# Packed half tiles in the down stage, grouped part copies of the weights, and a reordered opening

## What is computed

```
xn = layernorm(x)
gate = xn @ Wg.T ; up = xn @ Wu.T          # 2752 x 1024 each
inter = silu(gate) * up                     # 4096 x 2752
ffn = inter @ Wd.T                          # Wd: 1024 x 2752
attn = xn + softmax(q q^T / sqrt(1024)) q   # q: 4 x 1024 per feature column
out = x + attn * silu(ffn)
```

## Time and profile before

| | |
|---|---|
| three runs | 2485.27, 2484.89, 2483.41 us, median 2484.89 |
| profiled execution | 2484.12 us, span 2482.3 us |
| PE busy | 2407.4 us, 97% of the span, 11214 matmuls |
| DVE, ACT, POOL busy | 65%, 41%, 3% |
| mean granted TensorE clock | 0.989 of full speed |

### The profile page before, as it was taken

How to read it: one execution, slowest core, us unless ns; L and a number is a source line. 1 busy time by engine, 2 the same in 40 slices (tenths; PEclk the granted TensorE clock), 3 DMA queues, 4 the chain that set the end, 5 groups by cost and what they waited for, 6 DMA issues and landing times.

```text
span 2482.3 us, 30225 instructions
## 1 busy us (share of the span) xinstructions
PE 2407.4 (97%) x11214; PEld 1107.6 (45%) x11214; DVE 1605.8 (65%) x2757; ACT 1006.0 (41%) x1145; POOL 83.4 (3%) x72
## 2 busy tenths in 40 slices
PE   2899999999999999999999999999999999999999
PEld 2444444444444444444444444444444444444444
DVE  8888787668998867788888886565422422421431
ACT  8877777777878443544445421110010000001001
POOL 0000000000000000000000000000010011001001
PEclk7899999999999999999999999999999999999999
DMA  6855776657766895566655544248867767777764
GB/s 244 258 173 181 246 250 205 199 178 255 247 237 213 282 360 194 174 218 216 217 193 197 200 146 142 94 181 316 322 259 315 298 245 290 301 284 287 299 258 165
DMA packets 172127, 579.52 MB, mean 233 GB/s; under 512 B 17648, under 2 KB 42912, under 8 KB 154188
## 3 DMA queue, kind: packets, MB, share of 16 engines
q1 hardware_dynamic: 136716, 289.21, 34.4%
q10 hardware_dynamic: 35264, 288.37, 29.9%
HBM read 388.76 MB, written 188.75 MB: 233 GB/s over the span
## 4 chain that ended last, share of the span: by engine, by line
PE 88%; DVE 4%; ACT 3%; issue 3%; DMA 2%; POOL 0%; SPq 0%; ACTq 0%; POOLq 0%; DVEq 0%
PE ps L1813 56%; PE ps L1958 31%; ACT arena L792 1%; DMA arena<-in_x 1%; PE ps L1886 1%; ACT arena L805 1%; PE ps L1767 1%; DVE arena L1334 0%; DVE arena L1265 0%; DVE arena L1423 0%; DVE arena L1308 0%; DMA arena<-in_gu 0%; ACT arena L957 0%; DVE arena L1355 0%; POOL arena L761 0%
## 5 line engine op out<-in xcount | busy, mean ns | idle before, releaser
L1813 PE MATMUL ps<-arena 128*128 128x512 f16 x7152 | 1554.0, 380 | 12.4 <-ACT arena L995 6.8
L1813 PEld LDWEIGHTS ps<-arena 128*128 128x128 f16 x7152 | 700.1, 98 | 853.6 <-ACT arena L995 7.3
L1958 PE MATMUL ps<-arena 128*128 128x512 f16 x3696 | 797.9, 379 | 0.0
L792 ACT ACTIVATE arena<-arena,bias_t 128x2048 f32<-128x2048 f32 (+3 forms) x288 | 525.0, 1830 | 79.8 <-DMA arena<-in_dn 68.7
L1958 PEld LDWEIGHTS ps<-arena 128*128 128x128 f16 x3696 | 361.6, 98 | 436.1
L1423 DVE TENSOR_TENSOR arena<-arena 128x512 f16<-128x512 f32 x364 | 243.2, 684 | 11.7 <-ACT arena L957 10.4
L1221 ACT ACTIVATE arena<-arena,e_d 128x512 f32<-128x512 f32 x48 | 34.6, 721 | 424.3 <-DVE arena L1732 219.4
L1005 ACT ACTIVATE arena<-ps,gate_back 128x512 f32<-128x512 f32 x84 | 57.1, 680 | 305.6 <-PE ps L1813 305.5
L761 POOL TENSOR_TENSOR arena<-arena 128x512 f32<-128x512 f32 x64 | 81.5, 1280 | 2384.6 <-DMA arena<-in_xt 2076.2
L1708 DVE SCALAR_TENSOR_TENSOR arena<-arena,sc 128x512 f32<-128x512 f32 x192 | 129.8, 744 | 0.0
L1015 ACT ACTIVATE arena<-arena,gate_back 128x512 f32<-128x512 f32 x84 | 60.4, 720 | 161.5 <-DVE arena L1596 152.1
(11 more groups left out here) (108 smaller groups left out, 1167.4 us busy)
## 6 DMA issues: line engine op xcount, KB each, us to landing
isc<-arena SPq DMA_DIRECT2D x308, 256.0 KB, 2.6
arena<-wdsc ACTq DMA_DIRECT2D x28, 2816.0 KB, 10.2
arena<-isc ACTq DMA_DIRECT2D x28, 2816.0 KB, 18.1
arena<-xnsc SPq DMA_DIRECT2D x48, 1024.0 KB, 8.6
wsc<-arena ACTq DMA_DIRECT2D x21, 1792.0 KB, 6.7
arena<-in_x SPq DMA_DIRECT2D x48, 512.0 KB, 5.6
arena<-in_gu ACTq DMA_DIRECT2D x43, 512.0 KB, 4.6
wdsc<-arena SPq DMA_DIRECT2D x77, 256.0 KB, 2.1
```

The lines of the kernel that those rows point to most:

```text
L792: a_.activation(buf, src, ACT.Prelu, bias=bias_t[:, i:i + 1], scale=scale, alpha=alpha).then_inc(ramps, 1)
L1813: ins = t_.matmul(ps[:, bank, :], wreg[:, b, w, wa, k, :], xreg[:, j, o, k, xa, :], start=start and (k, wa, xa) == (0, 0, 0), stop=stop an ...
L1958: ins = t_.matmul(ps[:, bank, :], ring_w[b][:, k, wa, g, :], ring_i[b][:, k, xa, :], start=first and (k, wa, xa) == (0, 0, 0), stop=r not ...
```

## The change

Five things change together.

1. **Packed half tiles.** In the down stage, for combinations 1, 2 and 3, the last slice's 64 live rows are put twice into the 128 rows. SP stores high parts of the results in rows 0 to 63 and low parts in rows 64 to 127 of one plane, and the weights' high part in both halves; so one matmul does high x high and high x low. The second matmul (low x high) has zeros in the other half. `TERMS[::2]` is two matmuls where there were three. There are some more stores of the last weight slice (semaphores `pack_out`) and a shorter load of the results.
2. **Grouped part copies.** `W_ORDER` becomes (4, 5), (0, 1), (2, 6), (3): high and low parts are made for two combinations at a time, by 4 instructions instead of 7 on each of ACT and DVE. The places in `W_AT`, `W_CUT` and in ACT's program follow. In step 3 only one of six ramps stays in front of `sil_a`, and five go behind the copies.
3. **Early sums.** The first two of four become one instruction over two blocks.
4. **Opening.** Early combination 3 is transposed on PE ahead of tiles 10 and 11, and copied out by ACT ahead of three ramps and of those tiles. In `along`, p7 is last of each row k = 0 to 2.
5. **Statistics.** Tiles 16 and 17 move from step 3 to steps 4 and 5, tile 18 to the end of step 5, and 19 to step 6. SP's loads move with them.

```diff
-W_ORDER = [0, 4, 5, 6, 1, 3, 2]
+W_ORDER = [(4, 5), (0, 1), (2, 6), (3,)]
...
-STAT_AT = {3: {0: 16, 3: 17}, 4: {5: 18}, 5: {5: 19}, 6: {1: 20, 3: 21}, 7: {0: 22, 3: 23},
+STAT_AT = {4: {4: 16}, 5: {4: 17, 5: 18}, 6: {1: 19, 3: 20, 5: 21}, 7: {1: 22, 3: 23},
...
-W_AT[3] = [(2, i) for i in (4, 5, 6, 7, 9, 8, 10, 11, 12)] + [(3, i) for i in range(4)]
+W_AT[3] = [(2, i) for i in (4, 5, 6, 7, 8, 9)] + [(3, i) for i in range(4)]
...
-        W_AT[_s] = [(_u + 1, i) for i in (4, 5, 6, 7, 9)]
+        W_AT[_s] = [(_u + 1, i) for i in (4, 6, 7, 5)]
...
+PACKED = (1, 2, 3)
+ZEROS = {1: (1, 2), 2: (), 3: (3,)}
...
+                    if c[1] == last and o in PACKED:
+
+                        sp.dma_start(wdsc[o, 0:RR, last, :, :], src[RR:P]).then_inc(pack_out[o], 16)
+
+                        for to in ZEROS[o]:
+                            sp.dma_start(wdsc[to, RR:P, last, 1, :], src[0:RR, 1, :]).then_inc(pack_out[o], 16)
+                        src, dst = src[RR:P, 0, :], wdsc[o, RR:P, last, 0, :]
...
+                    if c[0] == "i" and c[1] == last and o in PACKED:
+
+                        src, dst = src[RR:P], isc[c[2], o, :, last, 0, :].rearrange("(s p) t -> p s t", s=2)
...
+                    if n == 1:
+                        for k in (4, 5):
+                            sp.wait_ge(st_out[k], 16 * SLOT.count(k))
...
+            def w_high(u, n):
+
+                ops = W_ORDER[n]
+                act.wait_ge(w_it, w_base(u, 6, 1) + [4, 1, 6, 2][n])
...
+                a_.activation(w_dest(u, ops, 0), w_source(u, ops), ACT.Copy).then_inc(w_hi, 1)
...
-            for o in (6, 1, 3, 2):
-                w_high(0, o)
+            for n in (2, 3):
+                w_high(0, n)
+            early_evac(3)
             for n in range(9, 12):
                 ramp(1, n)
...
-            early_evac(3)
             early_high(3, 0)
...
             p1_copy(0)
-            w_high(1, 0)
             for n in range(13, 16):
                 ramp(1, n)
             sil_a(0)
-            for o in (4, 5, 6, 1, 3, 2):
-                w_high(1, o)
+            for n in range(4):
+                w_high(1, n)
...
-                    ramps_of(s, 0, 2)
+                    ramps_of(s, 0, 1 if s == 3 else 2)
...
-                    for o in ([0, 4, 5], [6, 1, 3, 2])[j]:
-                        w_high(u + 1, o)
+                    for n in ([0], [2, 3])[j]:
+                        w_high(u + 1, n)
...
+                elif 4 <= s < 40 and u + 1 != LAST and not j:
+                    w_high(u + 1, 1)
...
-                v_.tensor_tensor(early_t[:, 1, :], b[:, 0, 1, :], b[:, 0, 0, :], ALU.subtract).then_inc(ep_made, 1)
-                v_.tensor_tensor(early_t[:, 3, :], b[:, 1, 1, :], b[:, 0, 1, :], ALU.subtract).then_inc(ep_made, 1)
-                dve.wait_ge(ep_made, 4 * e + 1)
+                v_.tensor_tensor(early_t[:, 1:4:2, :], b[:, :, 1, :], b[:, 0, :, :], ALU.subtract).then_inc(ep_made, 1)
+                dve.wait_ge(ep_made, 3 * e + 1)
...
-                    for name in FIRST:
+
+                    for name in FIRST if k == 3 else sorted(FIRST, key=lambda p: p == "p7"):
...
-                        for wa, xa in TERMS:
+
+                        packed = k == NDOWN - 1 and OPERAND[DOWN_ORDER[r]] in PACKED
+                        for wa, xa in TERMS[::2] if packed else TERMS:
```

More of the change, by code:

```diff
@@ L136 @@
     if _j == 0:
-        W_AT[_s] = [(_u + 1, i) for i in (4, 5, 6, 7, 9)]
+        W_AT[_s] = [(_u + 1, i) for i in (4, 6, 7, 5)]
     else:
-        W_AT[_s] = [(_u + 1, i) for i in (8, 10, 11, 12)] + [(_u + 2, i) for i in range(4) if _u + 2 < LAST or i == 0]
-W_AT[40] = [(LAST, 6)]
+        W_AT[_s] = [(_u + 1, i) for i in (8, 9)] + [(_u + 2, i) for i in range(4) if _u + 2 < LAST or i == 0]
+W_AT[40] = [(LAST, 4)]
 STORE_W_AT = {0: 1, 3: 2, 40: LAST}
@@ L292, in build @@
         sa, sb_ = carve(172, 2), carve(174, 2)
+        sums = carve(172, 4)
         blk = carve(176, 8).rearrange("p (r a t) -> p r a t", r=2, a=2)
@@ L395, in build @@
         w4_in = sem("w4_in")
+        pack_out = {o: sem(f"pack_out{o}") for o in PACKED}
         prod = sem("prod")
@@ L600, in store_stage @@
                 n = STAGED[c + (o,)]
+                src = stage[SLOT[n]]
+                last = NDOWN - 1
                 if c[0] == "d":
@@ L1057, in _ @@
             early_high(1, 1)
-            for o in (0, 4, 5):
-                w_high(0, o)
+            for n in (0, 1):
+                w_high(0, n)
             ramp(1, 8)
@@ L1176, in _ @@
                 if s == 3:
-                    for o in (1, 3, 2):
-                        w_high(2, o)
-                ramps_of(s, 0 if s == 4 else 3 if late else 2, 4)
+                    for n in (2, 3):
+                        w_high(2, n)
+                ramps_of(s, 0 if s == 4 else 3 if late else 1 if s == 3 else 2, 4)
                 if job:
@@ L1398, in slot_free @@
                     dve.wait_ge(st_out[SLOT[n]], 16 * SLOT_USE[n])
+                    held = next(c for c, k in STAGED.items() if k < n and SLOT[k] == SLOT[n] and SLOT_USE[k] == SLOT_USE[n] - 1)
+                    if held[:2] == ("d", NDOWN - 1) and held[2] in PACKED:
+                        dve.wait_ge(pack_out[held[2]], 16 + 16 * len(ZEROS[held[2]]))
                 elif SLOT[n] >= NSLOT:
@@ L1652, in _ @@
             early_made(1)
-            for i in (4, 5, 6, 7, 9):
+            for i in (4, 5, 6, 7):
                 w_item(0, i)
@@ L1657, in _ @@
             early_made(2)
-            for i in (8, 10, 11, 12):
+            for i in (8, 9):
                 w_item(0, i)
@@ L1664, in _ @@
             first_half(0)
-            for i in (1, 2, 3, 4, 5, 6, 7, 9):
+            for i in range(1, 8):
                 w_item(1, i)
@@ L1783, in early_transposes, with w_group @@
                     ins.then_inc(et_done, 1)
+            def w_group(o):
+                return [o in ops for ops in W_ORDER].index(True)
             def early_group(o):
@@ L1829, in _ @@
             early_transposes(0)
-            for e in range(1, 4):
-                early_transposes(e)
-                for tt in (6 + 2 * e, 7 + 2 * e):
-                    half_tile(tt, 0)
-                    half_tile(tt, 1)
+            early_transposes(1)
+            for tt in (8, 9):
+                half_tile(tt, 0)
+                half_tile(tt, 1)
+            early_transposes(2)
+            early_transposes(3)
+            for tt in (10, 11, 12, 13):
+                half_tile(tt, 0)
+                half_tile(tt, 1)
             def free_bank(s, name):
```

78 lines of the change are left out of this document (39 added, 39 removed).

## The result

Twelve runs of the changed kernel have a median of 2478.95 us (2476.07 to 2480.59), twelve of the kernel before, taken beside them, 2484.7 us. The ratio is 0.9978, 95% interval 0.997 to 0.9986: 5.75 us faster where 11.4 were forecast, and 1.5 us above the forecast's range. The profiled execution took 2479.32 us.

The account below looks back on a forecast made before the run. PE was taken as the bound, busy 2407.4 of 2482.3 us. Packing -10.4, opening +1.4, steps 4 to 6 -0.6 and later waits -1.0 summed to -10.6, from 2484.12 to 2473.5 us, range 2468.5 to 2477.5.

Parts of the forecast that it names:

- Grouped copies: Opening, early sums of e = 4: waiting for a pair's second member costs +0.9 us, one copy less gives back 0.5.
- Statistics out of step 3: Step 4: 2.55 us leave DVE ahead of p4's add, closing PE's 2.70 us wait; with 1.87 slow clock, 4.4 us earlier.
- no wait over 0.5 us: Sign at the add of p4 in step 4: PE waits there no longer than 0.5 us.
- Later waits: Behind 250 us: shorter waits for evacuations and `sil_a`, ACT's saved copies against 0.5 us more DVE; -1.0 us, bounds 0 and 2.
- Packing -10.4: Down stage: 48 matmuls less at 0.2158 us each, -10.4 us; loads stay hidden with 9.5 us spare per turn, new stores covered.
- The opening +1.4: Step 1: PE's wait for ACT's copy of p1 ends 1.4 us later, from 1.0 + 0.9 - 0.5.
- the moved combination: Opening: early combination 3 moved ahead delays the first products by 0.4 us, slow clock up to 1.7 more; taken as +1.0.
- Steps 4 to 6: Net -0.6 us: `sil_a` of step 4 2.5 us earlier, 1.9 of slow clock charged; ends -4.4 and +1.9.
- codes that land as late as before: Sign of being wrong, codes for u = 4 ahead of step 6; they were taken to come 2.0 us earlier.
- the opening loses: Rival, 13%: moved copy costs 2.7 us, waits at p4's add and `sil_a` stay over 2.7; -5.4, 2478.7 us (2476 to 2480).
- Packing brings nothing: Rival, 5%: the down stage goes at the pace of its loads, fewer matmuls only make PE wait; 2484 us.
- Slower: Rival, 5%: DVE's pair between adds of p7 and p5 in even steps holds back p5's bank and PE; 2500 us.

Follow-up runs that it names:

- e_pack_stat: Kernel before plus the packed half tiles and the moved statistics, without grouping and with the old opening; 2472.31 us, ratio 0.9955.
- e_pack: Kernel before plus the packed half tiles, their stores and waits, and nothing else; 2473.29 us, ratio 0.9962.
- e_open: Changed kernel with early combination 3 transposed and copied where it was before; 2476.79 us, ratio 0.9971.
- e_pack_open: Kernel before plus packed half tiles, moved early combination 3 and p7 last, without grouping, old statistics; 2475.18 us, ratio 0.9966.
- e_ramps: e_open with pair (2, 6) of step 3 earlier, first high pairs ahead of step 3's ramps, three ramps ahead of `sil_a`; 2475.27 us, ratio 0.9965.
- e_stat: Changed kernel with the statistics back at their old places; 2479.95 us, ratio 0.9986.
- e_fix26: Changed kernel with pair (2, 6) of step 3 one slot earlier, ahead of the add of p4; 2478.74 us, ratio 0.9982.

## Why the prediction was wrong, and what in it was right

**The step that failed is "Grouped copies".** It says that a pair has to wait for its second member, and prices this at the early sums of e = 4 only, not for each pair and its first reader. Two later steps left it out and came out wrong.

"Statistics out of step 3" sized the wait in step 4 by the bank alone: 2.55 us leave DVE ahead of the add of p4, the wait is 2.70, so it closes. The add did come earlier against PE's chain: at 158.87, though PE was 2.6 us later in step 1. But a product starts when its bank is free and its operands are there. Pair (2, 6) is due when p7 of step 4 needs its combination 6, and stood where combination 2 had stood: a wait of 4.25 us with 1.3 of slow clock behind it, where "no wait over 0.5 us" and "no half clock" were forecast. In the kernel without grouping the step holds: e_pack_stat has no wait at that add, no half clock, and a wait of 2.04 for `sil_a` with 1.7 of slow clock behind it.

"Later waits" took -1.0 us, from ACT's shorter list against 0.5 of DVE. It was +3.5, the largest error of the sum. Its rows follow below.

Term by term, forecast against the profiled execution, which took 5.8 us more than the 2473.5 of the sum:

- Packing -10.4: -10.8 behind the mark, -10 in e_pack, and 0.0038 by the ratio. Right, cover included.
- The opening +1.4: +2.6, PE's return in step 1. Of this the moved combination, +1.0 in the sum, made 1.8 (e_open) to 2.2 (e_pack_open) at step 1. The mechanism was named and the value taken too low; with 16 transposes at 3.65 us, the clock alone passed the upper bound of 1.7 in e_pack_open. The first products stood at 77.07, at the edge of the 75.4 to 77 forecast. Grouping in the opening, +0.9 and -0.5, was +0.4 forecast and about 0.6 shown (first products of e_open 0.5 later than in e_pack, step 1 later by 1.1). The wait in step 1 was 6.45, not 7 to 8, because the products ahead of it were late as well.
- Steps 4 to 6, net -0.6: the changed kernel is 2.6 late in step 1 and 2.5 late at the transposes of step 9, so this place gave -0.1. That the number came so near is luck, as neither of its waits was there: the wait was for the pair, and `sil_a` at 194.56 found PE still busy. The slow clock was charged at 1.87 a time; the row of 32.94 us holds 0.17 of the last matmul's end, so it was 1.7.
- Later waits -1.0: +3.5. From 254 to 450 us the changed kernel falls from 2.5 to 6.0 us behind. Of these 3.4 are the slow clock, twice 7.03 us for 24 matmuls that take 5.34.

The codes were part of the third term: 2.0 us were taken for the 1 MB of statistics that leaves the queue. They were asked for 2.6 us later (171.09), because the sums of u = 3 stand behind five ramps now. DVE of the changed kernel:

```profile
167.10 2.36 DVE L1338 TENSOR_TENSOR arena<-arena 128x1024 f32<-128x1024 f32 x2 [2.89 <-ACT arena L817]
```

They landed at 178.03, 1.4 us later than before, and the prediction had named codes that land as late as before as a sign of its being wrong. The megabyte is worth little that these traces can show: from issue to the first ramp it took 6.6 to 9.0 us in the five kernels that load the statistics there (7.7 on average), and 6.9 to 7.7 in the five that don't (7.1).

The later waits need their rows. DVE of the changed kernel near 412 us, and DVE and PE of before at the same place:

```profile
411.99 1.29 DVE L1455 TENSOR_TENSOR arena<-arena 128x512 f16<-128x512 f32 x2 [1.22 <-ACT arena L986]
413.20 1.22 DVE L1364 TENSOR_TENSOR arena<-arena 128x1024 f16<-128x1024 f32 x1
...
415.06 0.75 DVE L1584 SCALAR_TENSOR_TENSOR arena<-arena,up_back 128x512 f32<-128x512 f32 x1
```

```profile
407.57 1.29 DVE L1423 TENSOR_TENSOR arena<-arena 128x512 f16<-128x512 f32 x2 [0.28 <-ACT arena L957]
408.78 0.69 DVE L1301 TENSOR_TENSOR arena<-arena 128x512 f32<-128x512 f32 x1
...
410.10 0.74 DVE L1552 SCALAR_TENSOR_TENSOR arena<-arena,up_back 128x512 f32<-128x512 f32 x1
```

```profile
420.39 0.63 PE L1767 MATMUL ps<-id,arena 128*128 128x128 f32 x4 [1.22 <-ACT arena L962]
```

In the changed kernel DVE waits 1.22 us for ACT where it waited 0.28, as ACT has a pair and a ramp in front of the high part that DVE needs, and then makes a pair in 1.22 us where a sum of 0.69 (L1301) stood. The gated product (L1584, before L1552) starts 6.40 us after PE's `sil_a` wait ended at 408.66; before it was 4.92 us (410.10 to 405.18). ACT saves 0.6 us of this by its shorter list, and PE's wait for the transposes goes from 1.22 to 2.08 us. I had set ACT's saving against 0.5 us of DVE and missed the hand-over between them. The other of the two gaps, 2.09 us near 267, is not of the change's making: before it was 2.11, with 24 matmuls in 5.34 us behind it. That it was followed by a slow clock here is chance as far as these runs show, and so 1.7 of the 3.5 us is bad luck of the profiled execution.

Of the rivals, "the opening loses" is the one whose number came nearest: 2478.7 forecast, 2478.95 measured. That is luck. Its place was step 4 and its moved copy was right, but its reason was not: the wait at the add did close, a wait for an operand took its place, there was none over 2.7 us for `sil_a`, and it has no term for what happened behind 254 us. "Packing brings nothing" and "Slower" fell; after 430 us PE waits for nothing worth a row, and 2021.7 us behind the mark are the same to 0.1 in all six grouped kernels.

The Trainium skill, "VectorE: DVE Perf Modes", in the section on the TRN2 errata, favours one large operation over two small ones. The rows of the changed kernel agree about the instruction: 63 pairs of L1364 take 1217 ns each where two singles take 2 x 682. The kernels with these pairs are 4 to 4.5 us slower all the same, and e_ramps, which has the pairs and gets 3.9 us back at step 9, shows that most of it is the order of the work and not its duration.

**What stays open.** How the 4 to 4.5 us of grouping divide among its pairs, the ramps moved behind the copies and the early sums was not measured one at a time; e_ramps moves three things together. e_stat against the changed kernel, and e_open against it, differ by less than their intervals. For them the traces show the waits at each place, and no gain or loss in the total is shown.

## What to carry to other kernels

Matmuls that multiply zeros can be packed away at full price where PE is the bound: here 48 of them gave 10 us. When work is grouped, the group is due when its first member is needed and ready when its last one is; look up for each group who reads it next, before counting the saved instructions. And when a wait is to vanish, check every condition of the waiting instruction, the operands as well as the bank, and then the next wait in the chain: here each mended wait only uncovered another one, and of the kernels measured those without grouping have the lowest ratios (0.9955 to 0.9966), with only the reordered e_ramps level with them (0.9965).

## What the runs showed of the hardware

A short gap of TensorE sometimes costs more than itself. Over these ten traces there are sixteen gaps of 2.08 to 2.11 us ahead of four transposes and 24 matmuls, always at the same two places of the program. After six of them the 24 matmuls took 6.9 to 7.0 us, after ten 5.34. The clock granted in the changed kernel from 267.97 to 274.84 us was 0.75, a mixture of its two levels of 1.2 and 2.4 GHz; in e_pack from 263.75 to 268.93, at the same place behind a gap of 2.11, it was 1.00. Both happen at one place in kernels that differ nowhere near it. e_ramps, behind such a gap:

```profile
263.84 7.03 PE L1847 MATMUL ps<-arena 128*128 128x512 f16 x24
```

At the first place it was two of ten, at the second four of six. None of the gaps of 1.2 us at the second place (before and the three kernels without grouping) did it, but a gap of 2.04 us in e_pack_stat did and one of 3.30 us in e_fix26 did not. So the growth of a wait from 1.22 to 2.08 us costs 0.9 us, and in four of six traces 1.6 to 1.7 more. Whether this makes the 4.5 us between the fastest and the slowest run of the changed kernel (2476.07 to 2480.59) is not shown. Its two fastest runs had its highest mean granted clock, 0.994, but the two fastest of e_open had 0.988, under the 0.994 of slower ones. The Trainium skill, "TensorE: Matmul & The Clock Gate", Part 1, calls the monitor that sets this clock free-running, and its effect different from run to run; six of sixteen like gaps agree with that.
